# Attention steps and feed-forward pieces placed engine by engine beside a selective scan, with one more decay and one more h buffer and the output LN on ScalarE

## What is computed

```python
# 1. selective state space layer (mamba), then x1 = layernorm(x + it)
xz = einsum('ble,de->bld', layernorm(x), W_in); u, z = halves of xz          # 512 channels each
u = silu(causal_conv4(u)); dt_in, B, C = split(u @ W_x.T)                    # 16, 16, 16
dt = softplus(dt_in @ W_dt.T + dt_bias)
h_t = exp(dt * A) * h_{t-1} + dt * B * u        # for 512 channels x 16 states, over 512 steps
y = (sum over states of h * C + u * D) * silu(z);  x + y @ W_out.T
# 2. three rounds of slot attention on the 64 context rows, a GRU on the 512 tokens, then layernorm
sn = rmsnorm(slots); scores = (sn @ Wq.T) @ (Pn @ Wk.T).T * SCALE
attn = softmax(scores, over the 512 tokens); attn /= its sum over context rows
slots = gru_cell(attn @ (Pn @ Wv.T), slots)
# 3. feed-forward with spikes, then layernorm
y = square(relu(x @ W_fc.T)) @ W_proj.T; count of spikes in 5 steps / 5
```

## Time and profile before

| what | value |
|---|---|
| median of 3 executions | 1865.69 us |
| the profiled execution | 1863.23 us, its span 1861.2 us, clock granted to TensorE 0.849 of full |
| busy, PE | 1366.2 us, 73% (5472 matmuls) |
| busy, DVE | 1350.9 us, 73% |
| busy, ACT | 987.5 us, 53% |
| busy, POOL | 898.0 us, 48% |
| chain that ended last | PE 40%, DVE 31%, ACT 15%, issue 6%, POOL 5% |
| product by C on POOL, L443 | 256 of 2391 ns, 611.7 us |
| scan on DVE, L1078 | 256 of 2283 ns, 584.6 us |
| decay on ACT, L875 | 512 of 711 ns, 335.6 us |
| product on DVE, L1069 | 256 of 1229 ns, 314.6 us |

### The profile page before, as it was taken

The page is one execution under the profiler, slowest core; times in us unless marked ns, Lnnn a source line. Parts: engine busy times, 40 slices in busy tenths (PEclk is TensorE's granted clock), DMA queues, the critical chain, the costliest instruction groups (busy, mean ns, idle before and its releaser), DMA issues.

```text
span 1861.2 us, 16320 instructions
## 1 busy us (share of the span) xinstructions
PE 1366.2 (73%) x5472; PEld 826.3 (44%) x5472; DVE 1350.9 (73%) x1509; ACT 987.5 (53%) x1519; POOL 898.0 (48%) x459
## 2 busy tenths in 40 slices
PE   5555767686797758885778667887588857786975
PEld 2344344453455335552456334553355434562433
DVE  3987588957876888867888687867878778773142
ACT  4432665547663655647554655637465566534532
POOL 0665077615764266624666165642667155651110
PEclk9555978897899879998799978998799978998988
DMA  5632343205330532206321343305332153310000
GB/s 182 241 124 79 100 163 118 86 26 214 113 109 27 189 108 102 80 24 204 113 101 56 120 136 114 106 23 183 102 112 79 36 193 112 112 34 0 12 0 23
DMA packets 64762, 188.89 MB, mean 101 GB/s; under 512 B 6224, under 2 KB 22480, under 8 KB 64720
## 3 DMA queue, kind: packets, MB, share of 16 engines
q1 hardware_dynamic: 64720, 188.37, 29.3%
HBM read 183.62 MB, written 4.72 MB: 101 GB/s over the span
## 4 chain that ended last, share of the span: by engine, by line
PE 40%; DVE 31%; ACT 15%; issue 6%; POOL 5%; DMA 2%; ACTq 0%; DVEq 0%; POOLq 0%; SPq 0%; another core or an unknown queue 0%
DVE reg_a L1078 16%; DVE pb L1069 8%; PE py L645 6%; PE pc L631 5%; PE pc L623 4%; PE pb L486 4%; PE pb L605 3%; POOL reg_a L443 3%; ACT reg_a L875 2%; PE px L549 2%; PE px L527 2%; DMA x_out<-reg_m 2%; PE pb L587 2%; ACT xs L778 2%; DVE reg_m L927 1%
## 5 line engine op out<-in xcount | busy, mean ns | idle before, releaser
L443 POOL TENSOR_TENSOR reg_a<-reg_a,cb 128x1024 f32<-128x1024 f32 x256 | 611.7, 2391 | 438.1 <-DVE reg_a L1078 437.8
L1078 DVE TENSOR_TENSOR_SCAN reg_a<-reg_a,pb 128x1024 f32<-128x1024 f32 x256 | 584.6, 2283 | 143.5 <-ACT reg_a L875 110.2
L875 ACT ACTIVATE reg_a<-dt,neg_a 128x511 f32<-128x511 f32 x512 | 335.6, 711 | 165.3 <-DVE reg_a L1078 164.6
L645 PE MATMUL py<-ident,reg_a 128*128 128x128 f32 x2048 | 329.9, 318 | 70.6 <-POOL reg_a L443 70.6
L645 PEld LDWEIGHTS py<-ident,reg_a 128*128 128x128 f32 x2048 | 288.9, 167 | 167.6 <-POOL reg_a L443 104.9
L1069 DVE TENSOR_TENSOR pb<-bb,pb 128x1024 f32<-128x1024 f32 x256 | 314.6, 1229 | 29.7 <-ACT reg_y L835 2.6
L564 PE MATMUL pb<-ex,vw 64*128 64x512 f32 x48 | 46.9, 1075 | 146.9 <-DVE px L994 146.9
L623 PE MATMUL pc<-x2T,w_fc 128*128 128x512 f32 x224 | 119.0, 658 | 28.1 <-DVE reg_y L1095 21.2
L549 PE MATMUL px<-hT,whh 128*128 128x512 f32 x288 | 137.4, 613 | 0.4 <-ACT xs L778 0.4
L631 PE MATMUL pc<-w_pr,reg_m 128*128 128x256 f32 x448 | 109.8, 396 | 7.0 <-ACT y_sb L798 4.1
L405 POOL TENSOR_TENSOR xs<-xs,hT 128x1024 f32<-128x1024 f32 x24 | 56.6, 2358 | 96.2 <-ACT xs L786 96.2
(11 more groups left out here) (174 smaller groups left out, 2259.5 us busy)
## 6 DMA issues: line engine op xcount, KB each, us to landing
bb<-bc_rows SPq DMA_DIRECT2D x256, 512.0 KB, 3.7
cb<-bc_rows SPq DMA_DIRECT2D x64, 512.0 KB, 6.0
xin<-x_in SPq DMA_DIRECT2D x9, 512.0 KB, 3.6
xs<-x_in SPq DMA_DIRECT2D x8, 512.0 KB, 3.6
x_out<-reg_m SPq DMA_DIRECT2D x8, 512.0 KB, 3.4
w_in<-w_inT_in SPq DMA_DIRECT2D x1, 1024.0 KB, 7.1
w_fc<-w_fcT_in SPq DMA_DIRECT2D x1, 1024.0 KB, 10.9
w_pr<-w_prT_in SPq DMA_DIRECT2D x1, 1024.0 KB, 13.1
```

Source lines behind the costliest of these rows:

```text
L443: pool.tensor_tensor(h[:, g % HR], h[:, g % HR], cb[:, 2 * q:2 * q + 2], ALU.mult).then_inc(s["hc_done"], 1)
L645: mm = pe.matmul(py[:, cols_], h[:, g % HR, j, cols_], ident[:], is_transpose=True, start=(q == 0 and j == 0 and i2 == 0), stop=(q == PAIR ...
L875: ins = act.activation(d_a[:, g % 2, j, 1:], dt[:, c, 1:], ACT.Exp, scale=neg_a[:, c * NS + n + j:c * NS + n + j + 1])
L1078: dve.tensor_tensor_scan(h2[:, g % HR], d_a2[:, g % 2], pb[:, 1:3, :].rearrange("p a t -> p (a t)"), 0.0, ALU.mult, ALU.add).then_inc(s["s ...
```

## The change

1. `plan` is kept by engine: `place(position, *steps, on=ENGINES)`. A round at b takes the positions b to b+7, with its own table for PE, ACT, DVE and POOL, and DVE has half positions `("mid", g)` between scan g and product g+1.
2. The rounds begin at 2, 11 and 20 (before at "u", 9 and 20), the pieces have new positions, `ctx` 1 to 3 move to positions 0 to 2, `out_stats` to 0, `next_stats` to 15, `final 0` to 30.
3. `HR` is 4 and there are `DR` = 3 decay buffers. The room comes from `xp`, which now lies in the last `h` buffer.
4. Softplus of chunks 2 and 3 goes to position 0 (step `rest`). `dt_proj` writes to four banks of which two are no longer `pb` 1 and 2, so the first product has no wait for ACT's softplus, and PE's first sum has one instead.
5. The output layer norm's passes are four activations on ACT at position 3 with scale and bias; DVE makes the bias (`out_shift`, 128x4).
6. The store of `out` is issued after the 8th load of `bb` instead of after the 12th.

```diff
-HR = 3
+HR = 4
+DR = 3
+        xp = h2[:, HR - 1, 0:L]
+        dt_banks = (pb[:, 0, :], pc[:], py[:], pb[:, 3, :])
-        STORE_AT = 11
+        STORE_AT = 7
+        ROUNDS_AT = (2, 11, 20)
+        UNITS_AT = (4, 8, 9, 11, 13, 17, 19, 20, 22, 24, 27, 28, 29, 30, 31, 32)
+        def place_round(k, b):
+            for position, *steps in ((b + 1, ("norm", k), ("gate_h", k, 0)), (b + 3, ("colsum", k), ("gate_h", k, 1), ("spread", k)),
+                                     (b + 4, ("gate_x", k, 0), ("gate_x", k, 1), ("gate_h", k, 2)),
+                                     (b + 5, ("gate_h", k, 3), ("gate_x", k, 2), ("gate_x", k, 3), ("cand_h", k, 0)), (b + 6, ("cand_h", k, 1)),
+                                     (b + 7, ("cand_x", k, 0), ("cand_x", k, 1))):
+                place(position, *steps, on=("pe",))
+            for position, *steps in ((b, ("sq", k)), (b + 1, ("norm", k)), (b + 2, ("score", k)), (b + 4, ("gate_x", k, 0), ("gate_x", k, 1), ("reset", k)),
+                                     (b + 5, ("gate_x", k, 2), ("gate_x", k, 3)), (b + 6, ("keep", k)), (b + 7, ("cand", k))):
+                place(position, *steps, on=("act",))
+            for position, step in ((b + 1, ("score", k)), (("mid", b + 2), ("soft", k)), (b + 2, ("recol", k)), (("mid", b + 3), ("renorm", k)),
+                                   (("mid", b + 6), ("hold", k))):
+                place(position, step, on=("dve",))
+            for position, step in ((b + 5, ("keep", k)), (b + 6, ("cand", k))):
+                place(position, step, on=("pool",))
...
-                if q == 0 and c:
-                    pe.wait_ge(s["yt_ready"], c)
+                if q == 0:
+                    if c:
+                        pe.wait_ge(s["yt_ready"], c)
+                    else:
+                        pe.wait_ge(s["sp_abs"], 3)
...
+                elif step == "out_norm":
+                    act.wait_ge(s["out_shift"], 1)
+                    for i2 in range(TT):
+                        act.activation(acc.rearrange("p (i e) -> p i e", e=E)[:, i2], mem.rearrange("p (i e) -> p i e", e=E)[:, i2], ACT.Identity,
+                                       scale=stats["out"][3][:, i2:i2 + 1], bias=shift[:, i2:i2 + 1]).then_inc(s["out_norm"], 1)
...
-                    if g >= 2:
-                        act.wait_ge(s["scan_done"], g - 1)
+                    if g >= DR:
+                        act.wait_ge(s["scan_done"], g - DR + 1)
...
-                            act.wait_ge(s["dt_ready"], DT)
+                            act.wait_ge(s["dt_ready"], c + 1)
...
-                    else:
-                        dve.wait_ge(s["sp_abs"], 3)
```

More of the change, by code:

```diff
@@ L142, in decoder_layer @@
         cb = sb("cb", [P, NS, L])
-        xp = sb("xp", [P, L])
         bb = sb("bb", [P, HB, 2, L])
@@ L250, in decoder_layer @@
         plan = {}
-        def place(position, *steps):
-            plan.setdefault(position, []).extend(steps)
-        def place_round(k, positions):
-            parts = ([("sq", k)], [("norm", k)], [("score", k)], [("gate_h", k, 0), ("gate_h", k, 1)], [("soft", k)], [("colsum", k)],
-                     [("recol", k)], [("spread", k)], [("renorm", k)], [("gate_x", k, 0), ("gate_x", k, 1), ("reset", k)],
-                     [("gate_h", k, 2), ("gate_h", k, 3)], [("gate_x", k, 2), ("gate_x", k, 3), ("keep", k), ("cand_h", k, 0)],
-                     [("cand_h", k, 1)], [("hold", k)], [("cand_x", k, 0), ("cand_x", k, 1)], [("cand", k)])
-            for position, part in zip(positions, parts):
-                place(position, *part)
+        ENGINES = ("pe", "act", "dve", "pool")
@@ new lines, in place @@
+        def place(position, *steps, on=ENGINES):
+            for engine in on:
+                plan.setdefault((engine, position), []).extend(steps)
+        def place_round(k, b):
[12 more added lines that the diff above has]
+                place(position, step, on=("pool",))
```

99 lines of the change are left out of this document (55 added, 44 removed).

## The result

The changed kernel takes **1962.03 us** (median of 4 executions, 1959.32 to 1965.0), the kernel before in the same comparison 1864.74 (4 executions, 1863.43 to 1866.33). The ratio is 1.0522, 95% interval 1.0503 to 1.054: slower by 5.2%, where the prediction had 1778 us and faster.

A forecast was written before the change was run, and what follows sets the result against it. No engine is full, but DVE was taken to bound the scan loop. Batch starts 31.3, five full loops 47.0 and other loops 7, less 0.5 for the tail, gave 84.8 us off 1863.2: 1778 us, range 1735 to 1830.

The forecast's parts named there:

- its own signs: xp copy to scan 8.2 us; decay waits under 3; DVE busy 132 to 134; six table loads; loops 145 to 158.
- The start of a batch: From the copy of xp to the first scan: 4.15 us gained a batch, 31.3 us in all.
- the end of the loop: Behind the last scan: `out_proj` ends 13.2 us after it by either order, so `final 0` brings no gain there.
- The work of DVE in the loop: Scan loop: DVE's work falls from 133.3 to 132.4 us, 136.5 with hand-overs; output layer norm's passes save 5.2.
- The stalls that go: Scan loop: waits for decays and PE's sum vanish, through Ln ahead of Tanh, fewer table loads and more buffers.
- Rival 4: Deeper buffers do nothing, since ACT waits for PE, and the earlier start is lost on `bb`: 1863 us; chance 0.03.
- The stalls that stay or come: Attention rounds in a full loop: 13.9 us of DVE waits instead of 23.9, plus 1.5 for PE's clock.
- The chain at the restart of round 1: PE, ACT and POOL work ahead of round 1's Ln/Exp, the largest remaining stall: DVE waits 4.8 us.
- the clock's term: Round 1's restart: PE at half clock behind idling, bounds 0 and 4.4 us, taken as 1.5 a loop.
- Rival 3: Slower: PE runs at half clock after each round restart, 7 us a round, 21 a batch: 1898 us; chance 0.06.
- Rival 1: Stalls nearly vanish: 5 us of stall stay, a loop takes 142, the whole 1719 us; chance 0.18.
- The rule on table loads: ACT's table loads cost 1.28 us each, without the added drain of about 1.38 that would raise the sum 14 us.

The follow-up runs named there:

- experiment 2: The changed kernel with context steps 1 to 3 back in front of `x_proj` on all engines: 1883.47 us, ratio 1.0108 to the kernel before.
- experiment 1: The changed kernel with the load of `ctxt` and its wait issued behind the sixth load of `bb`: 1919.79 us, ratio 1.0293 to the kernel before.
- experiment 4: The changed kernel with the output layer norm's four passes on DVE again, at position 3: 1960.94 us, ratio 1.0521 to the kernel before.
- experiment 3: The kernel before with only three decay buffers, four `h` buffers and xp in the last of them: 1864.7 us, ratio 1.0003.
- experiment 9: Experiments 2, 5, 6 and 7 together, but with two decay buffers, three of `h` and xp in its own: 1823.45 us, ratio 0.9788.
- experiment 5: Experiment 2 with the fourth up piece at position 10 instead of 11: 1871.98 us, ratio 1.0038 to the kernel before.
- experiment 6: Experiment 2 with POOL's keep and candidate steps one position later: 1851.57 us, ratio 0.9929 to the kernel before.
- experiment 7: Experiment 2 with the finals where they were before and DVE's part of a down piece behind the last scan: 1855.32 us, ratio 0.9945.
- experiment 10: Experiments 2, 5, 6 and 7 together, plus the up pieces of positions 4 and 22 at 5 and 23: 1762.7 us, ratio 0.9455.

## Why the prediction was wrong

The sum gave -84.8 us and the profile has +96.3, a miss of 181. By the budget 92 of it lie between the loops and in the lead, 81.5 in the loops and 7.6 in the tail. Of its own signs, six table loads a batch, the loop's clock, DVE's busy time and the end of the waits for decays and sums came; the distance from the copy of xp to the scan (17.4 us and not 8.2) and the length of the loop (164.8, where over 158 was to mean wrong) did not.

**The start of a batch: the step that turned the sign.** The text says that xp is kept as before and that "The first `bb` was issued at 1053.79", and carries that issue over unchanged. I had followed ACT, PE and DVE and not SP, though the change moved a producer that SP waits for. The working of the step was otherwise good: with the queue free the distance from xp to the scan is 8.6 us (experiment 2) or 8.0 (experiment 1) against 8.2 forecast. What it left out are three things. First SP: the copy of xp to the scan takes 16.8 to 17.6 us, 62.6 us more in seven batches than 8.2 each. Second, that with ctx 1 to 3 ahead of it PE ran `x_proj` at its upper clock: 2.2 us in the batch shown, 16.8 in seven. "`x_proj` still waits for u", the text says, and takes its length for granted. Third, the end of the loop, costed at nothing ("which ends 13.2 us after the last scan by either order"): in the stretch shown `out_proj` ends 16.2 us after it (1060.2 to 1076.4), and over seven stretches the convolution starts 11.2 us later, a loss that stays in experiment 2 (10.7). The three are 90.6 of the 92 us; the rest is the lead, which gained 1.0 us of 2.3.

**The work of DVE in the loop: right.** Forecast 132.4 us, measured 132.52. The LN passes on ACT take 2.06 us, forecast 2.0. But experiment 4 shows that in the changed kernel the passes' place is worth nothing: work taken from an engine that then waits is no gain, and the sum booked all 5.2 us.

**The stalls that go: right in what goes, wrong in why and in what it brings.** The waits for decays and for PE's sum went. In experiment 3 the deeper rings take no decay wait away, and in experiment 9 the old rings bring only 0.2 us back; so the positions did it and not the buffers, as far as two other orders of the work can show for this one. Rival 4 had that half of the matter ("ACT waits for PE rather than for a buffer") and got 0.03.

**The stalls that stay or come: the term that was mis-sized.** Forecast 13.9 + 1.5 us a full loop, measured 27.6.

| wait | forecast | measured |
|---|---|---|
| score of rounds 0, 1, 2 | 1.5, 4.8, 2.2 | 0.4, 6.9, 4.6 |
| softmax Exps of rounds 0, 2 | 1.75, 2.4 | 1.9, 2.5 |
| hold | 1.1 | 2.0 |
| spread, three times | 0 | 3.9 |
| down piece ahead of the last scan | 0.2 | 5.0 |

The chain at the restart of round 1 was found with the right members; POOL's `keep` comes 4.6 us late to it and PE runs a part of it at the lower clock: sum 9 takes 1.97 us and up piece 03 2.84, where others in this loop take 1.04 and 1.88. That is 1.9 us, near the 1.5 of the clock's term; but the term counted this place alone. Ahead of the last scan a sum and a down piece take 1.97 and 3.36 us, where others take 1.04 and 1.89, and in round 0 a gate piece and the spread's matmuls 2.69 and 1.92, where the loop of 162.7 has 1.98 and 1.05: 4.0 us more. The 9 us that were missed almost whole, the spread behind a gate piece and the slot of the last scan, were places that I did not walk with times. Experiments 5, 6, 7 and 10 then show what edits at these places are worth: their waits were real, and the better version comes from them. Batch 2 was put at 149.9 us and took 164.5: it has no output LN, but all of the chains.

**The rivals.** Rival 3 had the sign. Its mechanism is only partly there. The loop's granted clock is 0.88, above the 0.85 of before, so PE was not slower over the loop than it had been; but three of the new waits have matmuls at the lower clock right ahead of them, the 5.9 us just named (1.9 and 4.0), where the rival had 21. Between the loops it cost 2.2 us at `x_proj`, and at `out_proj` 1.6 of the 2.8. The Trainium skill (TensorE: Matmul & The Clock Gate, Part 1) calls the throttled state the default; rows at 0.62 behind an idle PE agree. No rival named SP's queue, which is the larger part. Rival 1's loop of 142 us came only with experiment 10 (143.0), after five more edits, with `final 0` (3.2 us of DVE) out of the loop, and with 8.4 us of named waits where the rival had 5; the change by itself stayed far from it.

**The rule on table loads.** The changed kernel's load at 1188.12 takes 1.28 us, and the Ln behind it starts at 1189.41. The drain of 1.38 us that the Trainium skill (ScalarE: Activation LUTs, "What ACT_TABLE_LOAD costs") adds would put it at 1190.8; the rows don't show it, so taking 1.28 was right.

**What stays open.** Why experiment 1's loops are 20 us longer than the change's is known by its waits only. Why the clock granted at the same place differs from batch to batch in one execution isn't known. No run changed PE's clock alone, so its share of the loops' stalls is argued from rows.
